# Memory attention: a batch's own values projected with the tokens stationary, stored in DRAM by token, and loaded for each pair of batches

## What is computed

```
xn  = (x - mu) * rsqrt(var + EPS) * ln_g + ln_b
q   = split_heads(xn @ Wq)                 # 16 heads of 64
kv  = xn @ Wkv
k, v = split_heads(kv[..., :1024]), split_heads(kv[..., 1024:])
mem = split_heads(memories @ Wm)           # keys and values at once
k, v = concatenate([k, mem]), concatenate([v, mem])
attn = softmax(einsum('bhid,bhjd->bhij', q, k) * 64 ** -0.5)
out = einsum('bhij,bhjd->bhid', attn, v) -> (b, n, 1024) @ Wo + bo
```

## Time and profile before

| | |
|---|---|
| median of three runs | 2167.97 us (2165.10 to 2171.38) |
| span of the profiled execution, first to last instruction | 2168.2 us |
| TensorE busy with matmuls | 2077.7 us, 96% of the span |
| VectorE busy | 1272.0 us, 59% |
| ScalarE busy | 917.0 us, 42% |
| GpSimd busy | 73.3 us, 3% |
| projections, 1195.1 to 1326.7 us | TensorE busy 131.6 us |
| pair loop, from 1341.1 us on | some 600 us |
| mean granted clock of TensorE | 0.988 |

### The profile page before, as it was taken

One profiled execution on the slowest core, in us unless ns is written; L12 is line 12 of the kernel. 1 busy time (PEld: TensorE's weight loads), 2 busy tenths in 40 slices (PEclk: granted clock), 3 DMA queues, 4 the chain that ended last, 5 costly groups with the idle time before them and its releaser, 6 DMA issues. The chain is left out here.

```text
span 2168.2 us, 35911 instructions
## 1 busy us (share of the span) xinstructions
PE 2077.7 (96%) x14934; PEld 1510.8 (70%) x14934; DVE 1272.0 (59%) x2118; ACT 917.0 (42%) x2209; POOL 73.3 (3%) x111
## 2 busy tenths in 40 slices
PE   7999998999999999989999999999999999989999
PEld 6854454688768888534437887778778788775687
DVE  6446786743438888999997112443443543547563
ACT  4233432533333333899994332322322322333442
POOL 0000000000000000200000001000000000000122
PEclk9999988999999999999999999999999999999999
DMA  6300000211101011200021244211211211232001
GB/s 255 105 20 0 2 2 3 78 59 59 34 32 44 35 59 59 78 20 20 1 78 59 92 141 156 78 56 45 89 45 45 89 45 45 70 118 96 1 1 39
DMA packets 85073, 127.35 MB, mean 59 GB/s; under 512 B 7008, under 2 KB 48480, under 8 KB 84448
## 3 DMA queue, kind: packets, MB, share of 16 engines
q1 hardware_dynamic: 84912, 125.05, 17.4%
HBM read 110.10 MB, written 14.94 MB: 58 GB/s over the span
## 5 line engine op out<-in xcount | busy, mean ns | idle before, releaser
L1247 ACT ACTIVATE R<-bank 128x512 f32<-128x512 f32 (+3 forms) x151 | 89.3, 598 | 420.9 <-PE bank L928 336.3
L1513 ACT ACTIVATE R<-R 128x64 f32<-128x64 f32 x1024 | 247.5, 339 | 2.1 <-DVE R L2202 2.1
L928 PE MATMUL bank<-cth,wmh 128*128 128x512 f32 x512 | 207.7, 406 | 8.0 <-ACT arena L1617 6.5
L928 PE MATMUL bank<-cth,wml 128*128 128x512 f32 x512 | 202.1, 395 | 0.0
L928 PE MATMUL bank<-ctl,wmh 128*128 128x512 f32 x512 | 201.9, 394 | 0.0
L505 PE MATMUL bank<-XN,arena 128*128 128x512 f32 x320 | 145.4, 606 | 0.0
L505 PE MATMUL bank<-Y,arena 128*128 128x512 f32 x256 | 118.7, 610 | 3.3 <-ACT H L1556 3.3
L928 PEld LDWEIGHTS bank<-cth,wmh 128*128 128x128 f32 x512 | 96.1, 188 | 36.5 <-issue 15.3
L2313 DVE COPY Y<-bank 128x512 f32<-128x512 f32 x128 | 79.2, 681 | 59.7 <-PE bank L966 59.7
L928 PEld LDWEIGHTS bank<-cth,wml 128*128 128x128 f32 x512 | 96.1, 188 | 22.3
L928 PEld LDWEIGHTS bank<-ctl,wmh 128*128 128x128 f32 x512 | 96.3, 188 | 20.3 <-issue 0.2
(11 more groups left out here) (417 smaller groups left out, 4394.8 us busy)
## 6 DMA issues: line engine op xcount, KB each, us to landing
H<-in_ctxT SPq DMA_DIRECT2D x30, 512.0 KB, 5.1
arena<-in_L_attn_mlp_w SPq DMA_DIRECT2D x8, 1024.0 KB, 5.5
arena<-spill SPq DMA_DIRECT2D x32, 256.0 KB, 5.4
spill<-R SPq DMA_DIRECT2D x3, 2048.0 KB, 8.3
spill<-XN SPq DMA_DIRECT2D x3, 2048.0 KB, 8.3
arena<-in_L_ffn_Wg SPq DMA_DIRECT2D x4, 1024.0 KB, 7.4
arena<-in_L_ffn_Wu SPq DMA_DIRECT2D x4, 1024.0 KB, 5.2
arena<-in_L_ffn_Wd SPq DMA_DIRECT2D x4, 1024.0 KB, 5.9
```

The costliest lines, as they stand in the source:

```text
L928: last = mm(b[:, :].rearrange("p (a c) -> p a c", a=2), w_, c_[:, k, :, :], start=(k == 0 and n_ == 0), stop=(k == 3 and n_ == 2))
L1247: fn(dst, src, ACT.Copy).then_inc(act_bank_free, 1)
L1513: last = fn(EE[n % 3][:, a:a + 64], RC["Ey"][:, t, h, :], ACT.Copy, scale=RC["Ex"][:, t, h, 8 * j + x:8 * j + x + 1])
```

## The change

1. `dp_high` and `dp_low` get a second set (`_odd`), used by every other group. A piece is made in the first half of the group before its own and waits for the group two before.
2. The two `dv` groups hold a token tile of 128 stationary and stream the weights of 512 output features: `w_[:, :, k, :]`, which is 128 columns of each of the four pieces. The result has tokens on partitions. TensorE waits for all four pieces of such a group.
3. ScalarE copies these units into `stage_rows` (same places as `stage_out`), and SyncE stores a `dv` group with four transfers, 32 partitions each, to `value_rows` in DRAM: for each batch 33 rows of 1024, row 0 for the last key. Row 0 of all batches is stored once from `last_rows`.
4. For each pair SyncE loads the own keys into one of two buffers (one transfer of 256 KB), and each batch's 33 rows of `value_rows` straight into `vtail`, also in two buffers (two transfers of 33 rows of 4 KB). The wait ahead of them is now for the pair before last: GpSimd's copies and the weighted sums.
5. The tail transposes on TensorE, their copies on VectorE, GpSimd's two copies into `tail` and its memset go, as does GpSimd's wait for the tail transposes.
6. The waits for stores count the changed number of transfers. The program's scratch space for dynamic transfers is set to 1024, which leaves room for the second set of pieces.

```diff
@@ projections (TensorE)
+                    high, low = dp_high[g_ % 2], dp_low[g_ % 2]
+                    if w == "dv":
+                        pe.wait_ge(S["d_plo"], 4 * g_ + 4)
+                        for t in range(TT):
+                            b = open_act((w, half, t % 4, t // 4))
+                            for k in range(4):
+                                for i, (x_, w_) in enumerate(((dx_high, high), (dx_low, high), (dx_high, low))):
+                                    last = mm(b[:, :].rearrange("p (o n) -> p o n", o=4), x_[:, k, tl(t)], w_[:, :, k, :],
+                                              start=(k == 0 and i == 0), stop=(k == 3 and i == 2))
+                            last.then_inc(act_bank_full, 1)
...
@@ weighted (TensorE)
-                part(RDx["ptail"][64 * i:64 * i + 33, 0], RD["vtail"][64 * i:64 * i + 33, 0], False, 64 * i, True
+                if i == 0:
+                    pe.wait_ge(tail_full[bb // 2 % 2], 32 * (bb // 4 + 1))
+                part(RDx["ptail"][64 * i:64 * i + 33, 0], RD["vtail"][64 * i:64 * i + 33, bb // 2 % 2], False, 64 * i, True
@@ pair loop (TensorE)
-                for half in range(2):
-                    b = open_dve(("vtail", pr, half))
-                    for o in range(4):
-                        last = nc.tensor.transpose(b[:, tl(o)], RD["tail"][:, 4 * half + o, :], tab("ident"))
-                    last.then_inc(dve_bank_full, 1)
@@ d_piece_high (ScalarE)
-                    if n >= 4:
-                        act.wait_ge(*dp_used[n - 4])
+                    if n >= 8:
+                        act.wait_ge(*dp_used[n // 4 - 2])
...
@@ groups (ScalarE)
-                        if c == C2 - 1:
+                        if w == "dv":
+                            copy_out(stage_rows[g_ % 2][:, 4 * c + o, :], b[:, :])
...
+                        if c == 0:
                             d_piece_high(4 * g_ + o + 4)
@@ pair loop (VectorE)
-                for half in range(2):
-                    v.tensor_copy(RD["vtail"][:, 0, 512 * half:512 * half + 512], unit(("vtail", pr, half))[:, :]
-                                  ).then_inc(dve_bank_free, 1)
@@ GpSimd
-            g.memset(RD["tail"], 0.0).then_inc(S["d_zero"], 1)
...
-                pool.wait_ge(S["d_kv"], 32 * (pr + 1))
+                pool.wait_ge(k_full[pr % 2], 16 * (pr // 2 + 1))
...
-                if pr:
-                    pool.wait_ge(dve_bank_full, UV.at[("vtail", pr - 1, 1)] + 1)
...
-                g.tensor_copy(tail[:, :, :, 0:1], last_key)
-                g.tensor_copy(own[:, :, :, 1:33], RDa["kv"][:, 0].rearrange("p o (i t) -> p o i t", i=2))
-                g.tensor_copy(tail[:, :, :, 1:33], RDa["kv"][:, 1].rearrange("p o (i t) -> p o i t", i=2)
+                g.tensor_copy(own[:, :, :, 1:33], RDa["k"][:, pr % 2].rearrange("p o (i t) -> p o i t", i=2)
@@ load_pair (SyncE)
-                if pr:
-                    sp.wait_ge(S["d_self"], pr)
-                for w in range(2):
-                    sp.dma_start(RDa["kv"][:, w].rearrange("p (g o) t -> p g (o t)", g=2), spill[2 * w:2 * w + 2, pr].rearrange("g p n -> p g n")
-                                 ).then_inc(S["d_kv"], 16)
+                if pr >= 2:
+                    sp.wait_ge(S["d_self"], pr - 1)
+                    sp.wait_ge(dve_bank_full, UV.at[("pv", 2 * (pr - 2) + 1)] + 1)
+                sp.dma_start(RDa["k"][:, pr % 2].rearrange("p (g o) t -> p g (o t)", g=2), spill[0:2, pr].rearrange("g p n -> p g n")
+                             ).then_inc(k_full[pr % 2], 16)
+                for i in range(2):
+                    sp.dma_start(RD["vtail"][64 * i:64 * i + 33, pr % 2], value_rows[2 * pr + i]).then_inc(tail_full[pr % 2], 16)
@@ stores (SyncE)
+                if g_ == 0:
+                    sp.wait_ge(act_bank_free, UA.at[("mrow", 1)] + 1)
+                    sp.dma_start(value_rows[:, 0, :], last_rows[0:32, :]).then_inc(last_stored, 16)
                 sp.wait_ge(act_bank_free, UA.at[(w, half, 3, C2 - 1)] + 1)
...
+                if w == "dv":
+                    by_quarter = value_rows.rearrange("(t b) m n -> b m t n", b=4)
+                    for b4 in range(4):
+                        sp.dma_start(by_quarter[b4, 1:33, :, 512 * half:512 * half + 512], stage_rows[g_ % 2][32 * b4:32 * b4 + 32]
+                                     ).then_inc(spilled[g_ % 2], 16)
```

More of the change, by code:

```diff
@@ L163, in perceiver @@
             over(2 * 2048)
[L164 to L165 removed]
+            dp_high_even = shared_r("dp_high_even", [128, 4, 4, 128])
+            dp_low_even = shared_r("dp_low_even", [128, 4, 4, 128])
             wml = shared_r("wml", [128, 2, 4, 512])
@@ L231, in perceiver @@
         sums_full = [sem(f"sums_full{i}") for i in range(2)]
+        tail_full = [sem(f"tail_full{i}") for i in range(2)]
+        k_full = [sem(f"k_full{i}") for i in range(2)]
+        last_stored = sem("last_stored")
         stage_done = sem("stage_done")
@@ L364, in perceiver @@
         R2 = R[:, 10304:14400]
-        RD = region([("tail", (8, 128)), ("vtail", (1, 1024)), ("pt", (4, 512))], base=R2, limit=4096)
+        RD = region([("vtail", (2, 1024)), ("pt", (4, 512))], base=R2, limit=4096)
         RD["vt"] = Y[:, :, :]
@@ L375, in perceiver, with stored_groups @@
                      XNf.rearrange("p (b o t) -> p b o t", b=PAIRS, o=4)]
+        stage_rows = [R[:, 5152:5152 + 4096].rearrange("p (t n) -> p t n", t=TT), XNf.rearrange("p (t n) -> p t n", t=TT)]
+        def stored_groups(g):
+            return sum(16 * (4 if GROUPS[i][0] == "dv" else 1) for i in range(g % 2, g, 2))
         norms = H[:, 0, 2, 0:128]
@@ L954, in projections @@
                             last.then_inc(act_bank_full, 1)
-                            if c == C2 - 1:
-                                dp_used[n] = (act_bank_full, UA.n)
-                            elif n == 1:
+                            if c == 0 and n == 1:
                                 last_memory()
+                    dp_used[g_] = (act_bank_full, UA.n)
             def value_blocks(bb):
@@ L1644, in _ @@
                     for o in range(4):
-                        copy_out(stage_out[g_ % 2][:, 8 * c:8 * c + 8, o, :],
-                                 unit((w, half, o, c))[:, :].rearrange("p (b t) -> p b t", t=64))
-                        if c == C2 - 1:
+                        b = unit((w, half, o, c))
+                        if w == "dv":
+                            copy_out(stage_rows[g_ % 2][:, 4 * c + o, :], b[:, :])
+                        else:
+                            copy_out(stage_out[g_ % 2][:, 8 * c:8 * c + 8, o, :], b[:, :].rearrange("p (b t) -> p b t", t=64))
+                        if (c, o) == (0, 1) and g_ == 0:
+                            copy_out(RDm["m256"], unit("m256")[:, 0:256].rearrange("p (o b) -> p o b", o=8))
+                        if c == 0:
                             d_piece_high(4 * g_ + o + 4)
-                        elif 4 * g_ + o == 1:
-                            copy_out(RDm["m256"], unit("m256")[:, 0:256].rearrange("p (o b) -> p o b", o=8))
                 if g_ == 0:
@@ L2659, in _ @@
                 w, half = name
+                if g_ == 0:
+                    sp.wait_ge(act_bank_free, UA.at[("mrow", 1)] + 1)
+                    sp.dma_start(value_rows[:, 0, :], last_rows[0:32, :]).then_inc(last_stored, 16)
                 sp.wait_ge(act_bank_free, UA.at[(w, half, 3, C2 - 1)] + 1)
-                sp.dma_start(spill[g_].rearrange("b p n -> p b n"), stage_out[g_ % 2].rearrange("p b o t -> p b (o t)")
-                             ).then_inc(spilled[g_ % 2], 16)
+                if w == "dv":
[3 more added lines that the diff above has]
+                                     ).then_inc(spilled[g_ % 2], 16)
+                else:
+                    sp.dma_start(spill[g_].rearrange("b p n -> p b n"), stage_out[g_ % 2].rearrange("p b o t -> p b (o t)")
+                                 ).then_inc(spilled[g_ % 2], 16)
             for i in range(2):
-                sp.wait_ge(spilled[i], 16 * len(GROUPS) // 2)
+                sp.wait_ge(spilled[i], stored_groups(len(GROUPS) + i))
+            sp.wait_ge(last_stored, 16)
             sp.wait_ge(S["d_plo"], 4 * len(GROUPS))
```

36 lines of the change are left out of this document (21 added, 15 removed).

## The result

The changed kernel takes 2158.01 us (median of ten runs, 2154.80 to 2162.81), the kernel before 2171.28 us (ten runs on the same chip, 2165.10 to 2176.64). The ratio is 0.9941 with a 95% interval of 0.9930 to 0.9952: 0.59% faster, 13.3 us. Forecast were 2155.8 us within 2150 to 2163, and 12.2 us of gain.

A forecast was written before the change was run, and what follows sets the result against it. TensorE's stream was taken to bound the attention loop. Pairs 1 to 14 gain 14 x 0.87 = 12.2 us, other terms 0: span 2168.2 - 12.2 = 2156.0, less 0.2 to the median, 2155.8 us; range 2150 to 2163.

The forecast's parts named there:

- Transposes: Attention loop, pairs 1 to 14: removing eight TensorE transposes per pair gains 0.87 us each, 12.2 us in all.
- rival 1: All attention pairs: something else is late once the transposes go, so the gain becomes a wait; 2166 us, chance 0.08.
- End pairs: Pairs 0 and 15: the wait for exponentials grows and eats the gain; 0 taken, bounds 0 to 1 us gained each.
- Stationary tokens and strips: Value projection groups: holding tokens still and streaming weights in strips of 128 numbers keeps 389 ns per matmul; 0 us.
- a rival at 0.06: Value projection: strips slow 192 streaming matmuls by 0.22 us each, 42 us in all, giving 2198 us; chance 0.06.
- Buffers, GpSimd, VectorE: Second piece buffers in the projections, fewer GpSimd and VectorE copies in the pairs: none sets the pace; 0 us.
- Stores: Value groups' four transfers instead of one: hidden, as the buffer is wanted 21.9 us later; 0 taken, up to 5 lost.
- Loads of pair 0: Ahead of pair 0: less GpSimd work gains up to 0.38 us, later q loses up to 0.6; 0 taken.
- Code blocks: Attention loop: fewer instructions shift where TensorE's "issue" stalls fall, one or two more or fewer; plus or minus 3 us.

## Why the prediction was right, point by point

**Transposes, 14 x 0.87 = 12.2 us.** Right in size and place: 12.36 us over pairs 1 to 14, and 0.0 left when they are put back in all pairs. Taking the distance of starts (0.87) rather than the busy time (1.04) was the choice that mattered: 14 x 1.04 would have been 14.6 us.

**Kept, not turned into a wait (rival 1, 0.08).** Right. The pair-end wait stayed 0.94 us, since its chain starts from TensorE's own work. The new idle time in pairs 1 to 14 is 0.5 us in all: 1.9 us more for exponentials, 1.0 us less of "issue", and 0.4 us less in gaps too short to be listed.

**End pairs, 0 us, bounds 0 to 1 gained.** Pair 0 is exactly 0. The last pair lost 0.90 us in the profiled execution, outside the bounds, and this is the one step whose reasoning was incomplete. The wait grew as said (2.38 us for some 2.4), but I took a longer wait for a mere exchange with the transposes, and the granted clock can fall behind it (0.61 against 1.00, 1.7 us until the weighted sums). It isn't a steady loss: with the same wait and the clock at 1.00 the last pair took 23.64 us, 0.5 less than before, and that is within the bounds.

**Stationary tokens and strips, 0 us.** Right: 389 ns, projections 131.60 of 131.60. What stood as a rival at 0.06 is now priced: the strips would have to be much finer to cost anything, and even single numbers would leave the change about level with the kernel before.

**Buffers, GpSimd, VectorE.** Right at 0. The copies that VectorE lost are worth nothing (0.9936 with them, 0.9941 without), and the rest of the change adds up to nothing (0.9997 with the transposes back).

**Stores, 0, bound 5 us lost.** Right at 0. The working missed the issue side: I had counted bytes and landing time only, and SyncE spends 5.34 us on the four, so that the group has landed after 11.8 us and not 8.3. That is hidden here too, with 21.9 us of room.

**Loads of pair 0, between 0.38 gained and 0.6 lost, taken 0.** From the issue of the loads to the first scores it is 6.27 us (1337.24 to 1343.51), before 6.10 (1335.03 to 1341.13): 0.17 us lost, within the bounds. What comes last has changed: before, TensorE waited for GpSimd; now GpSimd is done at 1341.09 us, and q lands last, at 1343.31, 4.8 us after its issue (before 3.8), with the two tails' 0.81 us of issue ahead of it. With 37 rows it would have been 11 us; that kernel shows that this step stood on the number of rows.

**Code blocks, +-3 us.** TensorE's "issue" waits before weighted sums and score matmuls, up to the end of the loop, are 8.8 us (4.8 and 4.0) after and 10.8 (6.9 and 3.9) before: 2.0 us in favour of the change, within the bounds. In the last pair, one of them is larger (1.34 for 0.85 us) and one smaller (1.21 for 2.68), which hides a part of the clock's cost. The kernel with all transposes back has 7.9 us on these lines and a loop of 599.27, so they don't explain the gain. What moves them, these runs don't show.

**The total.** The loop gives 599.46 - 588.00 = 11.46 us: 12.36 from pairs 1 to 14, 0 from pair 0, -0.90 from the last (where another execution with the same wait and the clock at 1.00 gave +0.48). The medians differ by 13.3 us with an interval of 10.4 to 15.2. So the forecast of 12.2 and the loop's 11.46 both lie in it. The 1.8 us between loop and medians I can't place in full: without the last pair's 0.90 they would be 0.9, the stages ahead of the loop start it 2.4 us later in this profile, and the spread of runs is of the same size.

## What to carry to other kernels

Cost removed matmuls in a saturated stream by the distance of starts, and then walk from the place to the next wait behind it: a wait that hangs on the stream itself moves with it and keeps its length, one that is set by work that doesn't move eats the gain, and its growth can cost the clock besides. A constant wait at each turn of a loop is worth its own look even when the change at hand leaves it alone: here, reordering one engine's work and moving a quarter of one operation gave nearly as much again as the whole change (12.5 us after 13.3). And before a load gets another number of rows, ask which numbers divide it: 33 rows were free, 37 cost 11 us at the one place that was exposed.

## What the runs showed of the hardware that wasn't expected

- The clock behind a wait of TensorE at one place in the last pair: after 1.50 us and twice after 1.76 us the granted clock was 1.00. After 2.17 to 2.38 us it was 0.61 to 0.66 over the next 4.4 us in six kernels, and 1.00 in two (2.37 and 2.38 us). After 11.23 us ahead of pair 0 it was 0.50.
- The order of a moving operand of 128x512 in the rounded type: strips of 512 bytes 389 ns, of 16 bytes 437 ns, single numbers 451 ns; the stream's distance 0.227, 0.267 and 0.283 us.
- Four stores of 512 KB from 32 partitions each took SyncE 5.34 us to issue, one store of 2048 KB from 128 partitions 0.37 us. Each transfer lands 7.4 to 8.7 us (medians) after its own issue, but the fourth of the four lands 11.8 us after the first was issued.
- Loads of 37 rows of 4 KB left stretches of 27 GB/s with one sixteenth of the DMA engines busy (6.4%), and held up SyncE's next issues (7.49 us for two, otherwise 1.01); loads of 33 rows caused no such stretch.
- GpSimd takes 2.85 us for a subtraction of 128x512 into the rounded type, VectorE, at the same time, 1.76 us for 128x1536 of the same.
